# Gated cross-attention and ternary FFN on one core: 28 token tiles of 128, DMA transposes of heads and activations, half of the probability casts and the layernorm write on ScalarE, a hand-written opening order

## The chip, the cores and the metric

One core of one Trainium2 chip runs the whole program. The metric is the device time of one execution in microseconds (us); lower is better. The kernel before takes 1238.8 us, the median of 3 runs (1238.38 to 1241.94).

## The reference, cut to what matters

32 batches; in each, 112 query tokens `x` (256 wide) attend with 16 heads of 64 to 375 context tokens (256 wide). Then comes a feed-forward net with ternary weights and 8-bit activations, over tokens alone.

```
xn = layernorm(ctx) * w1 + b1;  k, v = split(xn @ Wkv)            # 375 x 2048 per batch
q  = (layernorm(layernorm(x)) * w2 + b2) @ Wq; q = q*(1+side) + side
p  = softmax(q k^T / 8);        x = x + tanh(g0) * ((p v) @ Wout) # 16 heads, 112 x 375
h  = act_quant(rmsnorm(layernorm(x))) @ ternary(W1)^T + b1        # 256 -> 1024
x  = x + tanh(g1) * (act_quant(rmsnorm(gelu(h))) @ ternary(W2)^T + b2)   # 1024 -> 256
```

Nothing behind the attention mixes tokens, so these 3584 tokens may be cut into tiles at any place.

## The kernel before, in words

Every float32 matmul operand is held as two float16 parts, a high one and the rest (`_h`, `_l`), and each product is three matmuls (`three`, L631). For each batch TensorE makes eight K jobs (128 rows of keys x 375), six V jobs (3 key tiles x 2 halves of 512 columns), two Q jobs, the transposes of the normalised inputs (Z0, Z1, ZX), eight score jobs S0 to S7 (two heads each, L644) and eight apply jobs A0 to A7 (probabilities times V, L656). Heads are transposed on TensorE (OO0, OO1) and go through Wout (WO); then the token steps follow: XT (transpose of the quantised x), F0 and F1 (first FFN layer), HT (transpose of the quantised hidden row), F2 (second layer). Each of the K, V, Q, Z, ZX, OO, WO, XT, HT and F jobs takes the next of four PSUM banks (`work`, `BANK` and `USE`).

Around them, for one pair of heads p: VectorE takes the row maximum (`M`, L561), ScalarE the exponential into float32 `prob` (`E`, L418), VectorE casts it to float16 into the first half of `pn` (`PH`, L568), GpSimd subtracts to get the low part (`PL`, L271), and SyncE issues one DMA transpose of `pn` (112 x 1536 float16) into `pt` (`T`, L211 to L217), which A of that pair reads. There are four `pn`/`pt` buffers and two of `prob`. The next S waits for E, since the score bank `ps_s` is single. K and V results leave PSUM in two steps: ScalarE writes the high part (`KH`, `VH`, L376), VectorE the low part (`KL`, `VL`, L498), and then the bank is free. GpSimd writes the layernorm result (`LNW`, L302 to L309) and splits q and z. Transposed heads leave PSUM through ScalarE (`OH`, L389) and VectorE (`OT`, L574); XT and HT leave through VectorE (`XTE`, `HTE`).

The order on each engine is a list written out by hand: `PE_ORDER`, `ACT_ORDER`, `DVE_ORDER`, `POOL_ORDER`, `SP_ORDER`, each a sequence of (step, batch offset) for one batch period, which `sequence` repeats for 32 batches with its ends cut off. All queues, SyncE's too, run strictly in their order: a step that waits holds everything behind it. Token steps run for each batch, that is for 32 tiles of 112 tokens, one to three periods behind the attention. Weight preparation (split in high and low, ternary rounding) is hung in front of named steps by `prepare` (L360, L474); GpSimd's `prepare_sides` (L259) waits for all small loads and for ScalarE's tanh.

Of the kernel before, what the change touches and what calls it, by code (L numbers as in the profile page):

```python
# [4 lines left out]
F16 = mybir.dt.float16  # L5
# [30 lines left out]
PE_ORDER = [  # L36
# [31 lines left out]
]  # L68

SP_ORDER = [  # L70
    ("T7", -1), ("T0", 0), ("T1", 0), ("T2", 0), ("LD", 3), ("T3", 0), ("T4", 0), ("RS", 0),
    ("T5", 0), ("ST", -3), ("T6", 0),
]
FIRST, LAST = -3, B + 2


def sequence(order):

    return [(name, it + off) for it in range(FIRST, LAST + 1) for name, off in order if 0 <= it + off < B]
# [3 lines left out]
for n, job in enumerate(j for j in sequence(PE_ORDER) if j[0][0] not in 'SA'):  # L83
    BANK[job], USE[job] = n % WORK_BANKS, n // WORK_BANKS + 1
HI_COUNT = {s: n + 1 for n, s in enumerate(s for s in sequence(ACT_ORDER) if s[0][0:2] in ("KH", "VH"))}


def build(nc, x, ctx, fside, g_x, g_f, ln1w, ln1b, ln2w, ln2b, wq, wkv, wout, w1, b1, w2, b2, out):
    from contextlib import ExitStack
    with ExitStack() as st:  # L90
# [13 lines left out]
        x1_b2 = stage[0:SQ, 0:B * D]  # L104
# [5 lines left out]
        ident, ident_h = sb("ident", [P, P]), sb("ident_h", [P, P], F16)  # L110
# [5 lines left out]
        b1_row, b2_row = sb("b1_row", [SQ, FF]), sb("b2_row", [SQ, D])  # L116
# [4 lines left out]
        ctx_bn, ctx_mv, ctx_ve, ctx_rs = sb("ctx_bn", [TP, TT, 6]), sb("ctx_mv", [TP, TT, 2]), sb("ctx_ve", [TP, TT]), sb("ctx_rs", [TP, TT])  # L121
        ctx_nm, ctx_nb = sb("ctx_nm", [TP, TT]), sb("ctx_nb", [TP, TT])
        x_bn, x_mv, x_ve, x_rs = sb("x_bn", [SQ, 6]), sb("x_mv", [SQ, 2]), sb("x_ve", [SQ, 1]), sb("x_rs", [SQ, 1])
        x_nm, x_nb = sb("x_nm", [SQ, 1]), sb("x_nb", [SQ, 1])
# [13 lines left out]
        ot_h, ot_l = sb("ot_h", [P, IC, SQ], F16), sb("ot_l", [P, IC, SQ], F16)  # L138

        x_res, x1 = sb("x_res", [SQ, D]), sb("x1", [SQ, D])  # L140
        x1_bn, x1_mv, x1_ve, x1_c = sb("x1_bn", [SQ, 6]), sb("x1_mv", [SQ, 2]), sb("x1_ve", [SQ, 1]), sb("x1_c", [SQ, 1])
        xc, xr, xq = sb("xc", [SQ, D]), sb("xr", [SQ, D]), sb("xq", [SQ, D], F16)
        amax1, clip1, inv1, qs1, deq1 = (sb(n, [SQ, 1]) for n in ("amax1", "clip1", "inv1", "qs1", "deq1"))
        xqt = sb("xqt", [P, KC, SQ], F16)
        hid_g = sb("hid_g", [SQ, FF])
        hid_r, hid = (stage[0:SQ, 8 * INNER + FF * i:8 * INNER + FF * (i + 1)] for i in range(2))
        hid_q = sb("hid_q", [SQ, FF], F16)
        ssq, inv_ff, eps_col, g_ms, g_ve, g_rs = (sb(n, [SQ, 1]) for n in ("ssq", "inv_ff", "eps_col", "g_ms", "g_ve", "g_rs"))
        amax2, clip2, inv2, qs2, deq2, deq2t = (sb(n, [SQ, 1]) for n in ("amax2", "clip2", "inv2", "qs2", "deq2", "deq2t"))
        hqt = sb("hqt", [P, FF // P, SQ], F16)  # L150
        y = sb("y", [SQ, D])
# [5 lines left out]

        wk_in, wv_in, wq_in, wout_in, w1_in, w2_in, ln_in, small_in = (sem(n) for n in ("wk_in", "wv_in", "wq_in", "wout_in", "w1_in", "w2_in", "ln_in", "small_in"))
        ctx_loaded, x_loaded, res_loaded, y_stored = (sem(n) for n in ("ctx_loaded", "x_loaded", "res_loaded", "y_stored"))

        consts_ready, gates_ready, side_ready, abs_ready, abs_summed, mean_ready = (sem(n) for n in (
            "consts_ready", "gates_ready", "side_ready", "abs_ready", "abs_summed", "mean_ready"))
        hi_split, lo_split, tern_rounded, tern_ready = (sem(n) for n in ("hi_split", "lo_split", "tern_rounded", "tern_ready"))
# [5 lines left out]
        ctx_stats, ctx_normed, z_ready = (sem(n) for n in ("ctx_stats", "ctx_normed", "z_ready"))  # L169
# [621 lines left out]
```

## Time and profile before

| | before |
|---|---|
| median of 3 runs | 1238.8 us |
| the profiled execution's own time | 1237.77 us |
| its span, first to last instruction | 1235.6 us |
| TensorE busy | 1131.4 us (92%) |
| VectorE busy | 1044.9 us (85%) |
| GpSimd busy | 875.2 us (71%) |
| ScalarE busy | 855.1 us (69%) |
| DMA transposes and loads (dynamic queue) | 118.42 MB, 53.4% of the 16 engines |
| mean granted TensorE clock | 0.98 |

Busy is the time in which at least one instruction of the engine ran. Matmuls are pipelined: one of 375 columns is shown with 0.32 us, while the next starts 0.16 us later, so the cost of a job on TensorE is read from start to start.

### The profile page before, as it was taken

The numbers are of one execution on the slowest core, as the hardware profiler recorded it, in microseconds if no ns is written. First come the engines' busy times: TensorE is split into PE (matmuls) and PEld (weight loads), VectorE is DVE, ScalarE is ACT, GpSimd is POOL, SyncE is SP. The second block draws the span as 40 slices with busy tenths as digits, with TensorE's granted clock in tenths as the row PEclk, the third lists the DMA queues.
The fourth block names the chain that finished last, engine by engine and source line by source line (L and its number), as shares of the span: only waits on it lengthen the run. The fifth ranks groups of instructions, "written<-read, shape, count | busy, mean of one in ns | idle before, by whom it ended". The sixth has DMA issues, their size and how long they took to land.

```text
span 1235.6 us, 32509 instructions
## 1 busy us (share of the span) xinstructions
PE 1131.4 (92%) x12354; PEld 768.6 (62%) x12354; DVE 1044.9 (85%) x2224; ACT 855.1 (69%) x1638; POOL 875.2 (71%) x1049
## 2 busy tenths in 40 slices
PE   2778999999999999999999999999999999999964
PEld 1455666666666666667666666766666666666643
DVE  2578898888888898888898888889888888998874
ACT  3455677777777677777777777777777777777742
POOL 4556787777777877777787777778777777877551
PEclk9899999999999999999999999999999999999986
DMA  8245554565555556554646565565655655464440
GB/s 255 44 89 85 99 87 99 102 102 95 109 93 96 91 103 102 97 110 90 104 85 103 100 102 105 93 106 88 100 101 103 98 103 94 87 104 90 85 89 11
DMA packets 381304, 120.48 MB, mean 98 GB/s; under 512 B 354976, under 2 KB 380016, under 8 KB 381152
## 3 DMA queue, kind: packets, MB, share of 16 engines
q1 hardware_dynamic: 381152, 118.42, 53.4%
q8 instruction: 99, 1.62, 0.6%
q14 instruction: 53, 0.43, 0.1%
HBM read 26.63 MB, written 3.67 MB: 25 GB/s over the span
## 4 chain that ended last, share of the span: by engine, by line
PE 44%; DVE 21%; ACT 11%; issue 10%; DVEq 6%; DMA 5%; POOL 3%; POOLq 1%; ACTq 0%
PE work L634 10%; PE work L636 9%; PE work L635 9%; PE ps_s L653 6%; DVE neg_max L561 5%; DMA pt<-pn 4%; DVE pn L568 4%; ACT prob L418 4%; PE ps_o L634 3%; ACT L418 2%; ACT k_h L376 2%; ACT hid_g L428 2%; DVEq L531 2%; DVE k_l L498 2%; PE ps_o L635 2%
## 5 line engine op out<-in xcount | busy, mean ns | idle before, releaser
L271 POOL TENSOR_TENSOR pn<-prob,pn 112x750 f16<-112x750 f32 x256 | 400.3, 1564 | 109.7 <-DVE pn L568 108.6
L418 ACT ACTIVATE prob<-ps_s,neg_max 112x375 f32<-112x375 f32 x512 | 266.0, 571 | 267.8 <-DVE neg_max L561 267.4
L561 DVE TENSOR_REDUCE neg_max<-ps_s 112x2 f32<-112x750 f32 x256 | 238.6, 932 | 17.1 <-PE ps_s L653 17.0
L568 DVE CAST pn<-prob 112x750 f16<-112x750 f32 x256 | 174.6, 682 | 67.0 <-ACT prob L418 66.8
L634 PE MATMUL work<-z,wkv_h 128*128 128x375 f16 x512 | 168.3, 329 | 37.2 <-DVE k_l L498 33.7
L634 PEld LDWEIGHTS ps_o<-v_h,pt 128*128 128x128 f16 (+1 forms) x1536 | 139.7, 97 | 87.9 <-issue 63.9
L634 PE MATMUL ps_o<-v_h,pt 128*128 128x65 f16 (+1 forms) x1536 | 171.8, 197 | 15.7 <-DMA pt<-pn 15.6
L635 PE MATMUL ps_o<-v_l,pt 128*128 128x65 f16 (+1 forms) x1536 | 169.8, 194 | 0.0
L636 PE MATMUL ps_o<-v_h,pt 128*128 128x65 f16 (+1 forms) x1536 | 168.5, 194 | 0.0
L636 PE MATMUL work<-z,wkv_l 128*128 128x375 f16 x512 | 167.1, 326 | 0.0
L635 PE MATMUL work<-z,wkv_h 128*128 128x375 f16 x512 | 166.8, 326 | 0.0
L376 ACT ACTIVATE k_h<-work 128x375 f16<-128x375 f32 x256 | 122.4, 493 | 37.2 <-PE work L636 37.0
L634 PE MATMUL work<-wkv_h,z 128*128 128x512 f16 (+1 forms) x384 | 146.2, 381 | 0.0
L635 PE MATMUL work<-wkv_l,z 128*128 128x512 f16 (+1 forms) x384 | 145.8, 380 | 0.0
L636 PE MATMUL work<-wkv_h,z 128*128 128x512 f16 (+1 forms) x384 | 145.7, 379 | 0.0
L636 PEld LDWEIGHTS ps_o<-v_h,pt 128*128 128x128 f16 (+1 forms) x1536 | 144.5, 98 | 0.0
L635 PEld LDWEIGHTS ps_o<-v_l,pt 128*128 128x128 f16 (+1 forms) x1536 | 144.1, 99 | 0.0
L498 DVE SCALAR_TENSOR_TENSOR k_l<-work,k_h 128x375 f16<-128x375 f32 x256 | 135.7, 541 | 9.4 <-ACT k_h L376 5.4
L498 DVE SCALAR_TENSOR_TENSOR v_l<-work,v_h 128x512 f16<-128x512 f32 (+1 forms) x192 | 131.9, 687 | 1.9 <-ACT v_h L376 0.3
L334 POOL TENSOR_TENSOR stage<-x,b_row 112x256 f32<-112x256 f32 x32 | 23.4, 732 | 143.3 <-DVE x L591 143.3
L376 ACT ACTIVATE v_h<-work 128x512 f16<-128x512 f32 (+1 forms) x192 | 112.6, 605 | 10.6 <-PE work L636 9.4
L653 PE MATMUL ps_s<-k_h,q_h 64*112 64x375 f16 x512 | 94.1, 364 | 17.6 <-ACT prob L418 17.1
(131 smaller groups left out, 2924.2 us busy)
## 6 DMA issues: line engine op xcount, KB each, us to landing
ctx_in<-in_ctx SPq DMA_DIRECT2D x32, 375.0 KB
pt<-pn SPq DMA_TRANSPOSE x256, 3.5
x_in<-in_x SPq DMA_DIRECT2D x32, 112.0 KB, 5.7
x_res<-in_x SPq DMA_DIRECT2D x32, 112.0 KB, 2.2
out<-y SPq DMA_DIRECT2D x32, 112.0 KB, 2.6
stage<-in_wkv SPq DMA_DIRECT2D x2, 1024.0 KB, 9.5
stage<-in_w SPq DMA_DIRECT2D x2, 1024.0 KB, 12.2
stage<-in_wq SPq DMA_DIRECT2D x1, 1024.0 KB, 9.3
```

What stands on the lines that cost most here:

```text
L271: g.tensor_tensor(pn[p % PBUF][:, 1, :, 0:SK], prob[:, p % 2], pn[p % PBUF][:, 0, :, 0:SK], ALU.subtract).then_inc(p_lo, 1)
L376: a.activation(dst, src, ACT.Identity, scale=1.0 / W_SCALE).then_inc(hi_done, 1)
L418: i = a.activation(prob[:, p % 2, h, :], ps_s[0:SQ, h, 0:SK], ACT.Exp, bias=neg_max[:, h:h + 1])
L428: a.activation(hid_g[:], hid[:], ACT.Gelu).then_inc(gelu_done, 1)
L498: v.scalar_tensor_tensor(out=dst, in0=src, scalar=1.0 / W_SCALE, in1=hi_part, op0=ALU.mult, op1=ALU.subtract).then_inc(evacuated[BANK[job] ...
L531: dve.drain()
L561: v.tensor_reduce(neg_max[:], ps_s[0:SQ, :, 0:SK], X, ALU.max, negate=True).then_inc(max_ready, 1)
L568: v.tensor_copy(pn[p % PBUF][:, 0, :, 0:SK], prob[:, p % 2]).then_inc(p_hi, 1)
L634: t_.matmul(dst, sh, mh, start=(n == 0), stop=False)
L635: t_.matmul(dst, sh, ml, start=False, stop=False)
L636: i = t_.matmul(dst, sl, mh, start=False, stop=(n == len(pairs) - 1))
L653: i = t_.matmul(ps_s[0:SQ, h, 0:SK], q[r, p, :], k[r, p, :], start=(n == 0), stop=(n == 2))
```

## The change

It does five things.

1. The token steps (RS, WO, X1 to YE, ST) run on 28 tiles of 128 rows, cut from the 3584 tokens without regard to the batch. `sequence` leaves out every eighth. `x_rows` and `out_rows` are the flat views; all `[SQ, ...]` tiles of these steps become `[P, ...]`.
2. The jobs OO0, OO1, XT and HT on TensorE are gone. ScalarE casts the heads from `attn` to `an` (`OH`), GpSimd subtracts the low part (`OL`), SyncE transposes both parts by DMA (`OT`) into a ring of 896 columns `ot_h`, `ot_l`. The quantised x and hidden tiles are transposed by DMA too (`XD`, `HD`), and VectorE clips them from SBUF to SBUF.
3. The casts `PH` of the pairs 0, 2, 4 and 6 run on ScalarE, those of 1, 3, 5 and 7 stay on VectorE.
4. The layernorm write `LNW` (three rows of 256 for the context, one for x) runs on ScalarE; GpSimd's power and product for context and x are one instruction each in place of two (`LNA`).
5. Each engine gets a list `FIRST` of its own for the opening, about two batches long, in which weight preparation and small constants are steps with a place of their own (`WKH`, `WQL`, `AS0`, `TN0`, `GT`, `SUM`, ...); then the new list `ORDER` repeats. In the opening SyncE loads Wk ahead of the small vectors and Wq ahead of the sides; gates and FFN biases are loaded with batch 1.

```diff
+NT = B * SQ // P
+RING = 7 * P
+CAST_ACT = (0, 2, 4, 6)
+ORDER["PE"] = [
+    ("Z1", 1), ("K5", 0), ("V00", 0), ("S0", 0), ("K7", 0), ("A4", -1), ("V02", 0), ("V01", 0),
+    ("A5", -1), ("S1", 0), ("K0", 1), ("A6", -1), ("Q1", 0), ("A7", -1), ("S2", 0), ("K1", 1),
+    ("V10", 0), ("ZX", 1), ("F0", -2), ("S3", 0), ("K2", 1), ("V11", 0), ("K3", 1), ("S4", 0),
+    ("F1", -2), ("A0", 0), ("A1", 0), ("V12", 0), ("K4", 1), ("S5", 0), ("WO", -1), ("A2", 0),
+    ("S6", 0), ("Q0", 1), ("A3", 0), ("F2", -3), ("Z0", 2), ("S7", 0), ("K6", 1),
+]
+ORDER["ACT"] = [
+    ("HR", -3), ("E0", 0), ("XR", -2), ("VH02", 0), ("KH7", 0), ("VH01", 0), ("PH0", 0), ("KH0", 1),
+    ("E1", 0), ("QF1", 0), ("KH1", 1), ("E2", 0), ("VH10", 0), ("ZXF", 1), ("OH1", -1), ("PH2", 0),
+    ("KH2", 1), ("E3", 0), ("VH11", 0), ("LNW", 2), ("KH3", 1), ("E4", 0), ("GE", -2), ("E5", 0),
+    ("PH4", 0), ("KH4", 1), ("VH12", 0), ("SQ", -2), ("E6", 0), ("QF0", 1), ("ZF0", 2), ("KH6", 1),
+    ("PH6", 0), ("E7", 0), ("KH5", 1), ("VH00", 1), ("OH0", 0), ("ZF1", 2),
+]
...
+ORDER["SP"] = [
+    ("XD", -2), ("T0", 0), ("T1", 0), ("OT0", -1), ("OT1", -1), ("LD", 3), ("T2", 0), ("ST", -4),
+    ("RS", -1), ("T3", 0), ("T4", 0), ("T5", 0), ("T6", 0), ("T7", 0), ("HD", -2),
+]
...
+    return [(name, b - b // 8 - 1 if name in TOKEN_STEPS else b) for name, b in steps if b % 8 or name not in TOKEN_STEPS]
...
+            def turn_heads(b, half):
+                sp.wait_ge(o_lo, 2 * b + half + 1)
...
+                for dst, part in ((ot_h, 0), (ot_l, 1)):
+                    sp.dma_start_transpose(dst[:, 4 * half:4 * half + 4, columns(b)],
+                                           an[half][:, part]).then_inc(o_turned[half], 16)
+            def turn_quantised(t):
+                sp.wait_ge(xq_ready, t + 1)
...
+                sp.dma_start_transpose(xqt_r[:], xq[:]).then_inc(x_turned, 16)
+            def turn_hidden(t):
+                sp.wait_ge(hq_ready, t + 1)
...
+                sp.dma_start_transpose(hqt_r[:], hid_q[:]).then_inc(h_turned, 16)
...
+            def split_heads(b, half):
+                pool.wait_ge(o_hi, 2 * b + half + 1)
+                g.tensor_tensor(an[half][:, 1], attn[:, half * HALF:(half + 1) * HALF], an[half][:, 0], ALU.subtract).then_inc(o_lo, 1)
...
+                    for t in range(TT):
+                        a.activation(ctx_n[:, t, :], ctx_in[:, t, :], ACT.Identity, bias=ln_nb[0:TP, t:t + 1], scale=ln_rs[0:TP, t:t + 1])
...
+                if name[0:2] == "PH":
...
+                    act.wait_ge(exp_done, g + 1)
...
+                    a.activation(pn[p % PBUF][:, 0, :, 0:SK], prob[:, p % 2], ACT.Identity).then_inc(p_hi_act, 1)
...
-                if name in ("OO0", "OO1"):
-                    pe.wait_ge(o_normed, 2 * b + 1 + int(name[2]))
-                    for m in range(4):
-                        c = 4 * int(name[2]) + m
-                        i = t_.transpose(w[:, m * SQ:(m + 1) * SQ], attn[:, c * P:(c + 1) * P], ident[0:SQ, 0:SQ])
```

## Rows read from the trace of the kernel before

**Rows 1.** Busy time by stage: engine busy us (instructions), granted clock, DMA share, GB/s.

```profile
0.00:49.50 49.50, 18.67 (x99) 10.28 (x100) 16.91 (x42) 15.77 (x25) 24.34 (x53) 0.90 0.57 172
49.50:128.00 78.50, 64.45 (x667) 41.50 (x666) 62.34 (x109) 44.32 (x90) 48.18 (x53) 0.96 0.49 83
128.00:1203.70 1075.70, 1033.11 (x11507) 705.33 (x11504) 951.11 (x2037) 785.75 (x1513) 797.48 (x935) 1.00 0.56 98
1203.70:1235.60 31.90, 15.18 (x89) 11.52 (x86) 14.50 (x37) 9.21 (x11) 5.17 (x9) 0.61 0.04 11
```

**Rows 2.** The same view for one period; order PE, PEld, DVE, ACT, POOL.

```profile
469.87:505.52 35.65, 34.72 (x388) 23.73 (x386) 31.61 (x70) 26.40 (x51) 27.04 (x33) 1.00 0.61 99
```

**Rows 3.** TensorE's waits between 128 and 1203 us: total us, times, longest.

```profile
PE work L634 <- DVE k_l L498: 22.3, 28, 1.7
PE ps_o L634 <- DMA pt<-pn: 15.6, 12, 3.2
PE ps_s L653 <- ACT prob L418: 4.3, 6, 1.4
```

**Rows 4.** TensorE's instructions in order of time, around 505 us: start, length, line.

```profile
500.13 0.55 PE L714 MATMUL work<-ident,attn 112*128 112x112 f32 x4
500.60 0.37 PE L653 MATMUL ps_s<-k_h,q_h 64*112 64x375 f16 x2
...
501.78 0.62 PE L734 MATMUL work<-w_t,xqt 128*112 128x512 f16 x2
502.23 0.32 PE L634 MATMUL work<-z,wkv_h 128*128 128x375 f16 x1
...
504.49 0.56 PE L727 MATMUL work<-ident_h,hid_q 112*128 112x112 f16 x8
504.97 0.37 PE L653 MATMUL ps_s<-k_h,q_h 64*112 64x375 f16 x2
...
506.15 0.29 PE L634 MATMUL work<-wout_h,ot_h 128*112 128x256 f16 x1
...
508.79 1.04 PE L740 MATMUL work<-w_t,hqt 128*112 128x256 f16 x8
509.76 0.37 PE L653 MATMUL ps_s<-k_h,q_h 64*112 64x375 f16 x2
```

**Rows 5.** ScalarE's instructions in order of time.

```profile
508.82 0.60 ACT L376 ACTIVATE v_h<-work 119x512 f16<-119x512 f32 x1
509.30 1.07 ACT L431 ACTIVATE stage<-hid_g 112x1024 f32<-112x1024 f32 x1
510.25 0.21 ACT L431 ACTIVATION_READ_ACCUMULATOR stage<-hid_g 112x1 f32 x1
...
526.67 0.60 ACT L422 ACTIVATE xr<-xc,round_col,qs 112x256 f32<-112x256 f32 x1
527.16 0.48 ACT L376 ACTIVATE k_h<-work 128x375 f16<-128x375 f32 x1
```

**Rows 6.** Two of VectorE's casts in order of time.

```profile
513.27 1.29 DVE L568 CAST pn<-prob 112x750 f16<-112x750 f32 x1
...
523.72 0.55 DVE L568 CAST pn<-prob 112x750 f16<-112x750 f32 x1
```

**Rows 7.** Groups of instructions: count, then busy us, mean ns, idle before.

```profile
L271 POOL TENSOR_TENSOR pn<-prob,pn 112x750 f16<-112x750 f32 x256 | 400.3, 1564 | 109.7 <-DVE pn L568 108.6
...
L568 DVE CAST pn<-prob 112x750 f16<-112x750 f32 x256 | 174.6, 682 | 67.0 <-ACT prob L418 66.8
...
L574 DVE TENSOR_TENSOR ot_l<-work,ot_h 128x448 f16<-128x448 f32 x64 | 39.3, 614 | 0.6 <-ACT ot_h L389 0.6
```

**Rows 8.** The tile pt: its DMA transposes, from issue to landing.

```profile
DMA to landing us min/median/max: 3.4/3.5/7.6
```

**Rows 9.** The page's DMA issues: KB each, median us from issue to landing.

```profile
x_res<-in_x SPq DMA_DIRECT2D x32, 112.0 KB, 2.2
```

**Rows 10.** The row maxima of all pairs: first and last start.

```profile
L561 DVE TENSOR_REDUCE neg_max<-ps_s x256: 921/929/941, 49.5 to 1194.8; 112x2 f32<-112x750 f32 x128
```

**Rows 11.** The chain that ended last, in the opening.

```profile
37.02 6.33 DMA ctx_in<-in_ctx
```

More of the change, by code:

```diff
@@ new lines, in sequence, with last_batch, columns, last_user @@
+def sequence(engine):
+    done = set(FIRST[engine])
+    steps = FIRST[engine] + [(name, it + off) for it in range(START, END) for name, off in ORDER[engine]
+                             if 0 <= it + off < B and (name, it + off) not in done]
+    return [(name, b - b // 8 - 1 if name in TOKEN_STEPS else b) for name, b in steps if b % 8 or name not in TOKEN_STEPS]
+def last_batch(t):
+    return (t * P + P - 1) // SQ
+def columns(b):
+    return slice(b * SQ % RING, b * SQ % RING + SQ)
+def last_user(b):
+    return [((b - 7) * SQ - 1) // P] if b >= 8 else []
@@ L88, in build @@
+CAST_COUNT = {(b, p): sum((i in CAST_ACT) == (p in CAST_ACT) for i in range(PAIRS)) * b
+              + sum((i in CAST_ACT) == (p in CAST_ACT) for i in range(p + 1)) for b in range(B) for p in range(PAIRS)}
 def build(nc, x, ctx, fside, g_x, g_f, ln1w, ln1b, ln2w, ln2b, wq, wkv, wout, w1, b1, w2, b2, out):
@@ L103, in build @@
         w2_f = stage[:, 10 * INNER:12 * INNER].rearrange("p (k n) -> p k n", k=FF // P)
-        x1_b2 = stage[0:SQ, 0:B * D]
+        RC = IC * RING // 2
+        ot_h, ot_l = (stage[:, RC * i:RC * (i + 1)].bitcast(F16).rearrange("p (c q) -> p c q", c=IC) for i in range(2))
+        x1_b2 = stage[:, 2 * RC:2 * RC + 4 * D].rearrange("p (s d) -> p s d", s=4)
+        hid_r, hid = (stage[:, 8 * INNER + FF * i:8 * INNER + FF * (i + 1)] for i in range(2))
         wkv_h, wkv_l = sb("wkv_h", [P, KC, 2 * INNER], F16), sb("wkv_l", [P, KC, 2 * INNER], F16)
@@ L235, in _ @@
                     store(b)
-            sp.wait_ge(y_stored, 16 * B)
+            sp.wait_ge(y_stored, 16 * NT)
         @block.gpsimd
@@ L386, in step @@
                 if name[0:2] == "OH":
[L387 to L390 removed]
+                    half = int(name[2])
+                    act.wait_ge(o_normed, 2 * b + half + 1)
+                    if b > 0:
+                        act.wait_ge(o_turned[half], 32 * b)
+                    a.activation(an[half][:, 0], attn[:, half * HALF:(half + 1) * HALF], ACT.Identity).then_inc(o_hi, 1)
                 if name[0:2] == "QF":
                     half = int(name[2])
+                    if b == 0:
+                        act.wait_ge(side_ready, 1)
                     act.wait_ge(full[BANK[job]], USE[job])
@@ L410, in step @@
                     i.then_inc(evacuated[BANK[job]], 1)
+                if name == "LNW":
+                    act.wait_ge(ln_ready, b + 1)
+                    if b > 0:
+                        for n in ("Z0", "Z1", "ZX"):
+                            act.wait_ge(full[BANK[n, b - 1]], USE[n, b - 1])
+                    for t in range(TT):
+                        a.activation(ctx_n[:, t, :], ctx_in[:, t, :], ACT.Identity, bias=ln_nb[0:TP, t:t + 1], scale=ln_rs[0:TP, t:t + 1])
+                    a.activation(x_n[:], x_in[:], ACT.Identity, bias=ln_nb[0:SQ, TT:TT + 1],
+                                 scale=ln_rs[0:SQ, TT:TT + 1]).then_inc(ctx_normed, 1)
                 if name[0] == "E":
@@ L461, in weight_means @@
             def weight_means():
-                dve.wait_ge(abs_summed, 1)
-                v.tensor_scalar(w_mean[:], ps_o[:, 0, 4 * VW:4 * VW + 2], 1.0 / (FF * D), 1e-5, ALU.mult, ALU.max)
+                bank = BANK["SUM", 0]
+                dve.wait_ge(full[bank], USE["SUM", 0])
+                v.tensor_scalar(w_mean[:], work[:, bank, 0:2], 1.0 / (FF * D), 1e-5, ALU.mult, ALU.max).then_inc(evacuated[bank], 1)
                 dve.drain()
@@ L715, in job @@
                 if name == "WO":
                     if b == 0:
-                        pe.wait_ge(lo_split, 4)
-                    results(b, ["OO0", "OO1"])
-                    i = three(w[0:SQ, 0:D], [(ot_h[:, c, :], ot_l[:, c, :], wout_h[:, c, :], wout_l[:, c, :]) for c in range(IC)])
-                if name == "XT":
-                    pe.wait_ge(xq_ready, b + 1)
-                    for c in range(KC):
-                        i = t_.transpose(wh[:, c * SQ:(c + 1) * SQ], xq[:, c * P:(c + 1) * P], ident_h[0:SQ, 0:SQ])
@@ L724, in job @@
-                if name == "HT":
-                    pe.wait_ge(hq_ready, b + 1)
-                    for c in range(FF // P):
-                        i = t_.transpose(wh[:, c * SQ:(c + 1) * SQ], hid_q[:, c * P:(c + 1) * P], ident_h[0:SQ, 0:SQ])
+                        pe.wait_ge(lo_split[3], 1)
+                    for half in range(2):
+                        pe.wait_ge(o_turned[half], 32 * (last_batch(b) + 1))
+                    r = slice(b % (RING // P) * P, (b % (RING // P) + 1) * P)
@@ L728, in job @@
+                    i = three(w[:, 0:D], [(ot_h[:, c, r], ot_l[:, c, r], wout_h[:, c, :], wout_l[:, c, :]) for c in range(IC)])
                 if name in ("F0", "F1"):
                     if b == 0:
-                        pe.wait_ge(tern_ready, 1)
-                    results(b, ["XT"])
+                        pe.wait_ge(tern_ready[0], 1)
+                    pe.wait_ge(x_clipped, b + 1)
                     c = slice(int(name[1]) * HALF, (int(name[1]) + 1) * HALF)
                     for k in range(KC):
-                        i = t_.matmul(w[0:SQ, :], xqt[:, k, :], w1_t[:, k, c], start=(k == 0), stop=(k == KC - 1))
+                        i = t_.matmul(w[:, :], xqt[:, k, :], w1_t[:, k, c], start=(k == 0), stop=(k == KC - 1))
```

407 lines of the change are left out of this document (212 added, 195 removed), and 70 rows, old and new, of tables (ACT_ORDER, CAST_ACT, DVE_ORDER, PE_ORDER).

## The prediction, made before the changed kernel was run

> **What bounds it now.** I cut the span into stages first, with the view of busy time by stage. Between 128 and 1203.7 us the kernel repeats 30 like periods, 1075.7 / 30 = 35.86 us each; ahead of them lie an opening of 49.5 us (to the first row maximum) and the first two batches with 78.5 us, behind them a tail of 31.9 us [rows 1, 10]. In the periods TensorE is busy 1033.11 / 30 = 34.44 us, at a granted clock of 1.00; in one typical period it is 34.72 of 35.65, against 31.61 for VectorE, 27.04 for GpSimd and 26.40 for ScalarE [rows 1, 2]. So TensorE is the bound, and not by appearance: its jobs stand start to start. The view of waits gives the remainder, 42.2 us in all or 1.4 us per period: 22.3 for VectorE's late low part of a K result, 15.6 for late transposes of probabilities, 4.3 for the exponential [rows 3]. The reader should see that the repeated part is worth 30 times whatever leaves TensorE, while opening and tail are chains of their own, in which TensorE works less than half the time.
>
> **TensorE's part.** From start to start [rows 4]: the transposes of one half of the heads take 500.60 - 500.13 = 0.47 us, two per batch 0.94; those of the hidden row 504.97 - 504.49 = 0.48; the two of the quantised x, by the same rate, 0.12. These 1.54 us go for every batch. WO takes 508.79 - 506.15 = 2.64 us, F2 0.97, F0 and F1 0.45 each: 4.51 us for a token tile. The 24 matmuls of WO take 0.11 us each for 256 columns, those of F0 0.225 for 512 [rows 4]: the time goes by the columns streamed, so I take a tile of 128 rows to cost what one of 112 does. One tile in eight is saved: 0.56 us per batch. Together 2.10 us; TensorE's need falls from 34.44 to 32.34 us per period.
>
> **The waits.** VectorE loses four of eight casts, 4 x 0.68, and two subtractions for the heads, 2 x 0.61 [rows 7]: 31.61 - 3.9 = 27.7 us of work, 83% of the new period, so the largest wait, for the low part of K, should shrink. What I set against it are ScalarE's new load and more transposes in SyncE's queue, so I let the wait fall only from 1.4 to 1.2 us. Period: 33.5 us. 30 x (35.86 - 33.5) = 71 us less; I round to 70. Bounds: waits of 0.4 us give 93 us less; waits of 2.4 us give 33 less.
>
> **ScalarE's part.** A cast of 750 elements lies between the 512-element row (start to start 0.48 us) and the 1024-element one (0.95) [rows 5]: 0.70 us, four times 2.8. The layernorm write is four rows of 256 with scale and bias per row, like the 0.49 us of `xr` [rows 5]: 2.0. The high part of the heads stays about what it was, and an eighth of the token steps goes, under 1 us. 26.40 + 4.8 - 0.8 = 30.4 us, bounds 29.5 (casts at 0.48) and 31.2 (no token steps saved): 88 to 93% of 33.5. It costs nothing in the sum as long as it hides under TensorE; it is the closest second, and the first rival.
>
> **GpSimd's part.** It gives up the layernorm write and gets two subtractions of 512 elements, at most 1.56 us each [rows 7]: 27.04 + 3.1 = 30.2 at the very most, still under 33.5. Nothing in the sum.
>
> A row bears on the casts: the same cast takes 0.55 us at 523.72 and 1.29 us at 513.27, where GpSimd's subtraction was running [rows 6]; the mean of 0.68 [rows 7] holds some of that, and ScalarE's copy should be free of it. The Trainium skill, in "SBUF — State Buffer", on the shared port pair, says that VectorE and GpSimd take one pair of ports as an exclusive lock and the loser blocks for the whole instruction, while ScalarE has its own. By that rule the trace's long casts are lock waits, and half of them go; this is the mechanism of the third rival, below.
>
> **DMA.** Eight pair transposes per period read 112 x 1536 float16 = 344 KB each, 2752 KB. Added are heads, 4 x 115 KB, and per token tile 66 and 262 KB, times 7/8: 746 KB, or 27% more. The DMA share of 0.56 [rows 1], all of it taken as transposes, becomes at most 0.56 x 1.27 x 35.9 / 33.5 = 0.76. Room is left. SyncE's queue is in order: XD stands ahead of T0 and waits for GpSimd's quantised x, the OTs stand ahead of T2 and wait for GpSimd's low part of the heads, HD stands behind T7 and waits for a GpSimd step of the next period, ahead of XD. Queued behind each are the pair transposes and the loads. Each A comes about four score jobs behind its T, some 16 us at 8 scores per period, less 3.2 us for maximum, cast and subtraction [rows 7, 10] and the exponential, against 3.5 us to landing [rows 8]; that cover hides the waits. If it is gone, a late landing costs TensorE its full delay (second rival below).
>
> **Opening.** Now VectorE stands at a statistic of batch 2 for 6.33 us while the load lands, and the first maxima wait behind it [rows 11]; the new order puts that step behind the first maximum. The layernorm write, Wq and the small loads leave the chain as well. I take 8.5 us (bounds 6, nothing but that wait, and 15). The first two batches take 78.5 us, 6.8 more than two periods [rows 1]; with new periods of 33.5, half of that excess kept, they take 70.4, 8 less (bounds 4.7 and 12). Together 16.5.
>
> **Tail.** Behind the last attention the three transposes by DMA stand in a serial chain. No row shows a small transpose; the nearest are 2.2 us to landing for a plain 112 KB load [rows 9] and 3.5 us for a pair transpose [rows 8]. I take 2.8 each, 8.4 us, and 1.2 for the new subtraction on GpSimd, less the TensorE transposes, which at the tail's clock of 0.61 take near twice the 1.07 us of one half of the heads, x and hidden, and less 0.6 for VectorE's subtraction: 9.6 - 2.0 - 0.6 = 7, bounds 5 and 10. The Trainium skill, "DMA: Bandwidth & Descriptors", in the anatomy of one DMA, gives a fixed part of about 2.0 us for any transfer; an estimate by it, 2.0 plus 115 KB at 436 GB/s, is 2.3 us a hop, and the sum would be 1.6 us lower. It speaks against small transposes on a serial path, and the trace of before, without any, can't say.
>
> **Sum.** 1237.8 (the profiled execution's own time: span 1235.6 and 2.2 around it) - 70 - 16.5 + 7 = 1158 us. That execution lies 1 us under the median of the runs; I forecast 1159.
>
> **Rivals.**
> - *ScalarE becomes the bound.* For: 30.4 us of work, two in-order queues (maximum, exponential) answering one another eight times per period; each exponential still waits for its maximum, as it waits now. If 4.2 us of idle time stay (half a microsecond per pair), the period is 34.6: 30 x 1.26 = 38 less, 1237.8 - 38 - 9.5 = 1190. Against: TensorE waits for the exponential 4.3 us in all now [rows 3], and a seventh more work need not change that.
> - *Slower than before.* SyncE's queue: XD, OT or HD waits for GpSimd, and the pair transposes behind it land late. The worst landing now is 7.6 us instead of 3.5 [rows 8]. Were one per period late on the path by these 4.1 us on top of the forecast, the period is 37.6 and the time 1237.8 + 30 x 1.74 - 9.5 = 1280. It decides the sign from 2.7 us per period on. Against: four buffers and a cover of over 10 us.
> - *The waits nearly vanish.* VectorE and GpSimd no longer collide in half of the casts, VectorE has 17% to spare; the waits fall to 0.4 us: 1237.8 - 93 - 9.5 = 1135.
> - *The repeated part does not move.* Another chain (maximum, exponential, cast, subtraction, transpose, apply) sets the period and only the opening pays: about 1228. Against: TensorE stands still for 1.4 us of 35.9 only.
>
> **Chances.** Forecast 0.61, ScalarE 0.18, waits vanish 0.13, does not move 0.04, slower 0.04. The forecast's own bounds are about 1145 to 1175. The range reaches down to 1134, through the third rival, and up to 1194, through the first. About 0.3% (4 us) is what a measurement of this kernel can tell from no change; faster takes all cases but the last and a sliver of the one before it.
>
> **What would show it.** Right: periods of 33.5 us with TensorE over 95% busy in them, no L714-like transposes of heads; the low-part wait under 15 us in all; first maximum near 41 us; ScalarE at 30 us per period; DMA share near 0.7; tail near 39 us. Wrong: TensorE's waits on ScalarE's exponential or on bank releases over 2 us per period (first rival), waits on `pt` that repeat in every period (second), or a period above 35 with TensorE under 93% busy.

## The result and the profile after

The changed kernel takes 1320.72 us (median of the runs, 1319.58 to 1324.64) against 1238.62 us for the kernel before beside it: ratio 1.066, interval 1.063 to 1.069. It is slower by 82 us; 1159 was forecast. The profiled execution has a span of 1317.8 us, against 1235.6.

The view of busy time by stage of the changed kernel, cut at the same places as [rows 1] (opening to the first row maximum, first two batches, repeated part, tail), with one late period in the last row but one; columns are the stretch, its length, busy us and instructions of PE, PEld, DVE, ACT and POOL, the granted clock, the DMA share and GB/s:

```profile
0.00:37.40 37.40, 17.05 (x99) 9.90 (x100) 17.01 (x36) 20.27 (x31) 16.15 (x37) 1.00 0.72 229
37.40:101.70 64.30, 57.22 (x593) 35.30 (x591) 52.29 (x93) 52.77 (x107) 44.50 (x43) 0.97 0.48 96
101.70:1277.10 1175.40, 1035.48 (x10890) 687.25 (x10888) 827.61 (x1754) 894.59 (x1718) 778.77 (x808) 0.94 0.57 109
1189.90:1224.70 34.80, 32.43 (x363) 21.46 (x363) 26.96 (x51) 28.41 (x55) 23.89 (x26) 1.00 0.54 114
1277.10:1317.80 40.70, 12.97 (x56) 7.08 (x56) 13.17 (x36) 9.30 (x11) 7.04 (x11) 0.58 0.18 43
```

| us | before | forecast | after |
|---|---|---|---|
| opening, to the first row maximum | 49.5 | 41.0 | 37.4 |
| first two batches | 78.5 | 70.4 | 64.3 |
| one period (of 30) | 35.86 | 33.5 | 39.18 |
| tail | 31.9 | 38.9 | 40.7 |

So the opening and the first two batches gave 26 us, 10 more than forecast; the tail took 9; and the repeated part, where 71 us were to be gained, lost 1175.4 - 1075.7 = 100 us. The question is the period alone. No engine has more work than was reckoned: per period VectorE is busy 27.6 us (forecast 27.7), ScalarE 29.8 (30.4), GpSimd 26.0 (30.2 at most). TensorE is the exception, 1035.48 / 30 = 34.5 us where 32.3 were forecast, with 617 fewer instructions than before and a clock of 0.94. And it waits. TensorE's waits in the repeated part, as in [rows 3] (total us, times, longest):

```profile
PE ps_o L765 <- DMA pt<-pn: 114.7, 30, 6.7
PE work L765 <- DMA stage<-an: 12.5, 16, 2.0
PE work L765 <- DVE k_l L616: 8.4, 19, 1.1
PE ps_s L784 <- ACT prob L551: 1.2, 1, 1.2
```

VectorE's late low part went from 22.3 to 8.4 us, the exponential from 4.3 to 1.2, as the forecast hoped. The wait for turned probabilities went from 15.6 us in 12 pieces to 114.7 in 30: once per period, 3.8 us. Instruction by instruction, 27 of the 30 stand ahead of the same job, A2, one in each of the batches 2 to 28. SyncE's queue in one period shows why:

```profile
583.55 1.23 SPq L327 DMA_TRANSPOSE hqt_r<-hid_q  x1
584.88 1.21 SPq L321 DMA_TRANSPOSE xqt_r<-xq  x1
586.78 6.13 SPq L304 DMA_TRANSPOSE pt<-pn  x2
593.00 5.80 SPq L314 DMA_TRANSPOSE stage<-an  x4
598.86 0.47 SPq L288 DMA_DIRECT2D ctx_in<-in_ctx  x1
599.37 0.53 SPq L289 DMA_DIRECT2D x_in<-in_x  x1
600.00 3.28 SPq L304 DMA_TRANSPOSE pt<-pn  x1
```

The order is T0 and T1, then the four transposes of the heads, the load of the next context and x, then T2. Each transpose of the heads holds the queue about 1.3 us, although it moves only 115 KB; T2 itself, right behind the load, holds it 3.28 us, where a pair transpose takes 1.34 in the median elsewhere. GpSimd has the low part of pair 2 ready well before that:

```profile
592.90 1.57 POOL L389 TENSOR_TENSOR pn<-prob,pn 112x750 f16<-112x750 f32 x1
```

It ends at 594.5; T2 is issued at 600.0. The chain of work that ended last goes the same way, and gives the second half of the delay (start, length, what):

```profile
591.58 1.33 SPq L304
593.00 1.21 SPq L314
...
600.00 6.46 DMA pt<-pn
...
638.56 7.12 DMA pt<-pn
```

The transposes of the other pairs take 3.1 to 4.3 us to landing; this one takes 6.46, and the one of the next batch 7.12. The table gives the median time from issue to landing of each pair's transpose, over the middle batches, worked out from the traces:

```
us        T0    T1    T2    T3    T4    T5    T6    T7   the load stands ahead of
before    3.5   3.5   3.5   5.7   4.5   3.5   3.5   3.5  T3
after     3.1   3.3   6.5   3.9   4.3   4.0   3.1   3.1  T2
```

[Rows 8] showed a median of 3.5 us and a worst of 7.6; sorted by place, the bad ones sit behind the 487 KB load. Third part: what the wait does to TensorE. The same view by stage, in small steps around the stall:

```profile
602.00:604.00 2.00, 0.89 (x9) 0.55 (x6) 0.73 (x2) 2.00 (x5) 0.65 (x1) 1.00 1.53 182
604.00:606.50 2.50, 0.00 (x1) 0.01 (x1) 0.00 (x0) 1.17 (x3) 2.43 (x2) 0.94 0.82 229
606.50:608.00 1.50, 1.50 (x22) 1.31 (x24) 0.00 (x0) 0.00 (x0) 0.75 (x2) 0.50 1.26 287
608.00:610.00 2.00, 2.00 (x24) 1.46 (x21) 1.17 (x2) 0.20 (x1) 0.00 (x0) 0.59 1.55 208
610.00:612.00 2.00, 2.00 (x39) 1.91 (x36) 1.83 (x5) 2.00 (x6) 0.00 (x0) 1.00 0.50 108
...
648.00:650.00 2.00, 2.00 (x25) 2.00 (x24) 1.95 (x4) 0.97 (x2) 0.00 (x0) 0.50 1.13 76
```

TensorE stands from about 603 to 606.5. When it starts again the granted clock is 0.50, the 1.2 GHz level, and it is back at 1.00 only after about 3 us; in the next period it starts again at 645.7 and is still at 0.50 from 648 to 650 (last row). So a stall costs its length and some work at half speed behind it. Wait and slow clock account for the period: 34.5 busy, and 139.5 / 30 = 4.65 of waits, is 39.2; of the 34.5, 2.2 are above the forecast and 1.8 above the 32.75 us that TensorE needs in the fastest kernel below, at a clock of 1.00.

One stall shows the wait by itself. Each row below runs from one start of A2 to the next, with one wait of 3.6 to 4.0 us in it. The first begins with a slow stretch. The second begins behind a wait of 3.46 us after which the clock stayed at 1.00, the only one of the 27:

```profile
606.50:645.70 39.20, 34.83 (x368) 22.98 (x368) 28.44 (x62) 30.89 (x59) 26.70 (x29) 0.94 0.64 115
884.33:922.85 38.52, 33.53 (x369) 21.95 (x369) 27.66 (x62) 30.83 (x59) 26.92 (x30) 1.00 0.56 113
```

TensorE is busy for 33.5 us there and for 34.8 with the slow stretch, with as many matmuls; in the other periods with a token tile it is 34.0 to 36.4. So even at full clock the period is far above the forecast: the wait is the larger part, and the clock adds up to 3 us.

One more thing speaks for the load as a partner: the last batches have nothing left to load. The row 1189.90:1224.70 above is a stretch of that kind: 34.80 us, 4.4 shorter than the mean period, at a clock of 1.00, TensorE busy for 32.43 of it, with the heads' transposes still in the queue. From first row maximum to first row maximum the periods of batches 29 and 30 take 34.6 and 34.7 us, and neither has a wait for turned probabilities.

### The profile page after: what moved, and what is told of

Its sections match the earlier page's. It is cut to its first block, busy times and chain, and to the rows that moved or that the text cites. A ratio compares the mean times of both kernels' runs of the same rounds, so it can differ in the third digit from the quotient of the medians.

```text
span 1317.8 us, 31456 instructions
## 1 busy us (share of the span) xinstructions
PE 1122.7 (85%) x11634; PEld 739.5 (56%) x11634; DVE 910.1 (69%) x1916; ACT 976.9 (74%) x1866; POOL 846.5 (64%) x897
## 4 chain that ended last, share of the span: by engine, by line
PE 34%; POOL 15%; DMA 12%; issue 9%; SPq 9%; DVE 7%; POOLq 6%; ACT 5%; DVEq 2%; ACTq 0%
DMA pt<-pn 11%; PE work L765 7%; SPq L314 7%; PE work L766 7%; PE work L767 7%; PE ps_s L784 6%; POOL pn L389 5%; POOLq L413 3%; PE ps_o L765 2%; POOL q_l L401 2%; POOL z L414 2%; POOL an L394 2%; PE ps_o L766 2%; PE ps_o L767 2%; ACT prob L551 2%
## 5 line engine op out<-in xcount | busy, mean ns | idle before, releaser
L765 PE MATMUL ps_o<-v_h,pt 128*128 128x65 f16 (+1 forms) x1536 | 180.2, 202 | 119.2 <-DMA pt<-pn 117.2
L765 PEld LDWEIGHTS ps_o<-v_h,pt 128*128 128x128 f16 (+1 forms) x1536 | 151.9, 102 | 140.9 <-DMA pt<-pn 123.1
L766 PE MATMUL ps_o<-v_l,pt 128*128 128x65 f16 (+1 forms) x1536 | 180.1, 200 | 0.0
L767 PE MATMUL ps_o<-v_h,pt 128*128 128x65 f16 (+1 forms) x1536 | 179.7, 201 | 0.0
L766 PEld LDWEIGHTS ps_o<-v_l,pt 128*128 128x128 f16 (+1 forms) x1536 | 151.6, 104 | 10.9
L767 PEld LDWEIGHTS ps_o<-v_h,pt 128*128 128x128 f16 (+1 forms) x1536 | 151.8, 102 | 0.0
L616 DVE SCALAR_TENSOR_TENSOR k_l<-work,k_h 128x375 f16<-128x375 f32 x256 | 138.4, 541 | 17.3 <-ACT k_h L477 16.9
L616 DVE SCALAR_TENSOR_TENSOR v_l<-work,v_h 128x512 f16<-128x512 f32 (+1 forms) x192 | 128.2, 681 | 1.2 <-ACT v_h L477 0.7
L477 ACT ACTIVATE v_h<-work 128x512 f16<-128x512 f32 x192 | 116.3, 606 | 6.3 <-PE work L767 4.0
L561 ACT ACTIVATE pn<-prob 112x750 f16<-112x750 f32 x128 | 106.9, 835 | 0.1
L441 POOL TENSOR_TENSOR x_c<-x_ve,minus_half 128x1 f32<-128x1 f32 x28 | 16.4, 587 | 139.7 <-DVE x_ve L647 139.7
L517 ACT ACTIVATE q_f<-work,side_add,side_mul 128x112 f32<-128x112 f32 x256 | 92.9, 446 | 14.5 <-PE work L767 14.5
```

What stands on the lines that cost most here:

```text
L477: a.activation(dst, src, ACT.Identity, scale=1.0 / W_SCALE).then_inc(hi_done, 1)
L517: i = a.activation(q_f[:, c, :], work[:, BANK[job], m * SQ:(m + 1) * SQ], ACT.Identity, bias=add, scale=mul)
L561: a.activation(pn[p % PBUF][:, 0, :, 0:SK], prob[:, p % 2], ACT.Identity).then_inc(p_hi_act, 1)
L616: v.scalar_tensor_tensor(out=dst, in0=src, scalar=1.0 / W_SCALE, in1=hi_part, op0=ALU.mult, op1=ALU.subtract).then_inc(evacuated[BANK[job] ...
L765: t_.matmul(dst, sh, mh, start=(n == 0), stop=False)
L766: t_.matmul(dst, sh, ml, start=False, stop=False)
```

## The experiments

All times are medians beside runs of the kernel before on the same chip (1236.8 to 1237.8 us). Period, opening and tail come from each trace, cut at the same events. The queue's list, SyncE's, is the place of most edits; the order of the changed kernel is `T0 T1 OT0 OT1 LD T2 ST RS T3 ...`. Rows of waits are cut at fixed times: 128 to 1270 us in the first and third run, 101 to 1270 in the second (SyncE's row), 128 to 1203 in the fourth, 104 to 1140 with the load split or late, 101 to 1120 in the last kernels. In the slower kernels they leave out one to five of the last periods.

**Which of the two steps ahead of T2: the load or the heads?** First only the load goes behind T2.

```diff
-("OT0", -1), ("OT1", -1), ("LD", 3), ("T2", 0),
+("OT0", -1), ("OT1", -1), ("T2", 0), ("LD", 3),
```

> The changed kernel with one move in SyncE's repeated list: the load of the batch three ahead (LD) goes behind the transpose T2 instead of ahead of it. Theory 1 (order in SyncE's queue): T2, which A2 waits for, is issued 6 us after its data are there and then lands in 6.5 us because 487 KB of load are under way; with LD behind it, it is issued 1 us sooner and lands in about 3.5, so the 3.8 us wait of TensorE ahead of A2 goes, and the period falls from 39.5 to about 35: some 1185 us, faster than both kernels. Theory 2 (the DMA engines or SyncE's queue have too much work in sum, 27% more transposed bytes): the order does not matter, over 1290 us. Theory 3 (ScalarE is overloaded, so everything on TensorE comes late): no change either, over 1290 us.

Measured: 1330.2 us, ratio 1.076 (1.074 to 1.078), period 39.46. Nothing gained. TensorE's waits in its repeated part, and from TensorE's timeline the instruction behind one of them (start, length, line, and in brackets the idle time before it):

```profile
PE ps_o L765 <- DMA pt<-pn: 118.0, 31, 5.8
```

```profile
614.87 0.23 PE L765 MATMUL ps_o<-v_h,pt 128*128 128x65 f16 x1 [5.25 <-DMA pt<-pn]
```

T2 now lands in 3.1 us, but T3, now right behind the load, in 7.1, and TensorE waits ahead of A3 instead of A2. The victim is whichever transpose follows the load.

Then both the load and T2 ahead of the heads:

```diff
-("OT0", -1), ("OT1", -1), ("LD", 3), ("T2", 0),
+("LD", 3), ("T2", 0), ("OT0", -1), ("OT1", -1),
```

> The changed kernel with LD ahead of T2 as it is, but the four transposes of the heads (OT0, OT1) behind T2. Theory 1, if the heads' transposes are what holds T2: T2 is issued some 3 to 5 us sooner, though still behind the load, and lands in 6.5 us; TensorE's wait ahead of A2 shrinks by about 3 us: period 36.5, some 1230 us. LD itself waits for the layernorm write of ScalarE, which may hold T2 in its turn. If the load's traffic is the larger part, this run gains less than the one with LD behind T2. Theory 2 and 3: over 1290 us.

Measured: 1419.52 us, ratio 1.147 (1.143 to 1.152), period 42.28. Worse, and the DMA queue's own waits, then TensorE's (104 to 1373 us), show why:

```profile
SPq L288 <- ACT x_n L542: 79.8, 27, 3.7
```

```profile
PE work L765 <- DMA stage<-an: 192.7, 27, 8.5
```

Moved forward, the load itself waits 3 us per period for ScalarE to have done with the input buffer (the layernorm write), which I had overlooked in the edit, and T2 and the heads stand behind it. T2 still lands in 6.6 us, but TensorE hardly waits for it any more (22.5 us in 9 pieces for all pairs): it waits ahead of WO for the heads. Two moves are mixed in this run, so it doesn't price either alone.

And T2 ahead of both:

```diff
-("OT0", -1), ("OT1", -1), ("LD", 3), ("T2", 0),
+("T2", 0), ("OT0", -1), ("OT1", -1), ("LD", 3),
```

> The changed kernel with T0, T1, T2 first, then the heads' transposes, then LD. Theory 1: T2 lands well before A2; but now the heads' transposes are issued 3 us later and WO, which stands ahead of A2 on TensorE, may wait for them instead: between 1175 (no new wait) and 1230 us (WO waits 1.5 us per period). Theory 2 and 3: over 1290 us.

Measured: 1321.69 us, ratio 1.069 (1.065 to 1.072), period 39.07. No gain:

```profile
PE work L765 <- DMA stage<-an: 83.6, 26, 4.7
PE ps_o L765 <- DMA pt<-pn: 39.2, 24, 4.9
```

Now the heads are late for WO, which is in TensorE's queue ahead of A2, and T3 lands in 6.2 us behind the load. In these three runs the loss only moved, or grew. None of the three orders of these steps helps: T2, T3 and the heads are each needed by TensorE soon.

**Does the load alone do it, without the rest of the change?** The kernel before, with the load one place earlier, ahead of T2 as in the changed one.

```diff
-("T1", 0), ("T2", 0), ("LD", 3), ("T3", 0),
+("T1", 0), ("LD", 3), ("T2", 0), ("T3", 0),
```

> The kernel before with LD moved ahead of T2, as the change has it, nothing else. If the load ahead of T2 alone costs the time, whatever stands in the queue besides, this is slower by over 2 us per period (over 1300 us). If it takes the heads' transposes in front of it too, there is room for it here: T2 then lands a few us later, still in time for A2: within 1% of 1238 us.

Measured: 1400.36 us, ratio 1.132 (1.130 to 1.134), period 41.13, and T2 lands in 6.4 us. The DMA queue's waits, then TensorE's:

```profile
SPq L204 <- POOL x_n L309: 178.6, 26, 7.2
```

```profile
PE ps_o L634 <- DMA pt<-pn: 119.3, 26, 5.2
```

One place of one step costs the kernel before 163 us, though here two things add: the load waits for the buffer (6.9 us each time, 26 times), so T2 is issued 4.6 us after its data (median), and T2 lands late behind it. No part of the change's new work is needed for this kind of stall.

**Is it the load's shape?** The context tile has 125 partitions, all transposes have 112. The load is split in 112 and 13 partitions, same bytes, same place (shortened; VectorE's wait for the load counts both parts).

```diff
-sp.dma_start(ctx_in[:], rows)
+sp.dma_start(ctx_in[0:SQ], rows[0:SQ])
+sp.dma_start(ctx_in[SQ:TP], rows[SQ:TP])
```

> The changed kernel with nothing moved: only the context load of 125 partitions is cut into two, 112 and 13 partitions. The runs so far say that a pair transpose issued right behind a load lands in 6.3 to 7.1 us instead of 3.1, wherever in the list that is. Theory 1a (the load's own time on the DMA engines is what the next transpose waits for, and it is long because 125 partitions spread over few engines): spread over more engines, the transpose T2 behind it lands in some 4.5 us, TensorE waits 2 us less ahead of A2 and keeps its clock: period 39.5 to about 37, some 1245 us. Theory 1b (the load is bound by memory or by its bytes, not by how it is spread): T2 still lands in 6.5 us, within 1% of 1320 us.

Measured: 1241.42 us, ratio 1.004 (1.002 to 1.006), period 36.78: 79 us less than the changed kernel, from one more DMA per batch. Some 72 of them are the period's, the rest the opening and the first two batches. T2 lands in 3.9 us instead of 6.5. What is left:

```profile
PE ps_o L770 <- DMA pt<-pn: 70.3, 39, 5.4
PE work L770 <- DMA stage<-an: 14.7, 18, 1.4
```

The Trainium skill, in "DMA: Bandwidth & Descriptors", on why a DMA increments its semaphore by 16, says that a transfer is dealt to the largest number of engines up to 16 that divides the slowest dimension of both its sides. By that rule 125 partitions go to 5 engines, 112 to 16 and 13 to 13. The traces agree. T2 lands in 6.5 us behind the whole load and in 3.9 behind the split one. And the packets of 1024 bytes, which are the rows of the two loads and of x, can be counted by their starts and durations: in the 9 us behind the issue of the whole load, the commonest number of them under way at once, while any is, is 5, in the kernel before and in the changed one; behind the split load it is 16.

The same split in the kernel before:

> The kernel before with its context load cut in the same way (112 and 13 partitions). There T3 stands behind the load and lands in 5.7 us, with room ahead of A3. Theory 1a: T3 lands in about 4.5 us and the time stays within 0.5% of 1238 us, since TensorE hardly waits for transposes there (15.6 us in all, of which some may go). Theory 1b: no change in landing.

Measured: 1226.5 us, ratio 0.992 (0.990 to 0.993). T3 lands in 4.0 us instead of 5.7, but the period goes only from 35.86 to 35.74; most of the 10 us come from the opening (49.5 to 42.7), where the first maxima waited for a load [rows 11]. In the kernel before the late T3 was just hidden: in the median it landed 0.2 us ahead of A3.

**Somewhere with more cover.** The load goes behind T4, three pairs later, with T2 and T3 ahead of it.

```diff
-("LD", 3), ("T2", 0), ("ST", -4), ("RS", -1), ("T3", 0), ("T4", 0), ("T5", 0),
+("T2", 0), ("ST", -4), ("RS", -1), ("T3", 0), ("T4", 0), ("LD", 3), ("T5", 0),
```

> The changed kernel with LD moved behind T4, to where no pair transpose is due for some 5 us; the load itself is unchanged. Theory 1 (a load just ahead of a transpose that TensorE is about to need): T2, T3 and T4 all land in about 3.1 us, T5 has its data later than the load's end; TensorE's wait on pt falls from 3.8 to under 1 us per period, its clock stays at 2.4 GHz, the period is about 34.5: some 1170 us. Theory 2 (too many transposes in sum) and 3 (ScalarE): over 1270 us.

Measured: 1240.61 us, ratio 1.002 (1.000 to 1.004), period 36.53. T5 behind the load takes 7.0 us, yet TensorE's wait for probabilities is down to 13.4 us. Another took its place: TensorE's waits, and VectorE's wait for the load.

```profile
PE work L765 <- DVE k_l L616: 41.5, 28, 3.0
PE work L765 <- DMA stage<-an: 22.5, 23, 1.6
PE ps_o L765 <- DMA pt<-pn: 13.4, 10, 3.2
```

```profile
DVE ln_bn L706 <- DMA ctx_in<-in_ctx: 75.1, 27, 4.9
```

Loaded this late, the context arrives after VectorE has come to its statistics; VectorE stands 2.8 us and the low part of K behind it is late. A faster load should cure just that, so both edits together:

> Both: LD behind T4 and the context load cut in two. Theory 1: as with LD behind T4 alone, or up to 1% less, since T5 may still meet the load's tail; some 1165 us.

Measured: 1184.05 us, ratio 0.958 (0.956 to 0.960), period 34.86. The view by stage, a stretch of 33.5 us in its middle with as many matmuls as a mean period (363), and TensorE's waits:

```profile
500.00:533.50 33.50, 32.66 (x363) 21.40 (x360) 25.72 (x61) 28.91 (x57) 26.28 (x28) 1.00 0.59 122
```

```profile
PE work L770 <- DMA stage<-an: 23.0, 23, 2.0
PE ps_o L770 <- DMA pt<-pn: 14.4, 12, 3.4
PE work L770 <- DVE k_l L621: 7.3, 13, 1.4
```

VectorE's wait for the load is 23.6 us. What remains first is the heads' transposes.

**The issue cost of the heads.** Both parts of a half are made one tile of 112 x 1024 and turned by one DMA instead of two (the ring of the transposed heads and the indices of WO follow).

```diff
-for dst, part in ((ot_h, 0), (ot_l, 1)):
-    sp.dma_start_transpose(dst[:, 4 * half:4 * half + 4, columns(b)],
-                           an[half][:, part]).then_inc(o_turned[half], 16)
+sp.dma_start_transpose(ot[:, 8 * half:8 * half + 8, columns(b)],
+                       an[half][:].rearrange("p a k -> p (a k)")).then_inc(o_turned[half], 16)
```

On top of the last kernel:

> On top of the kernel with LD behind T4 and the context load in two parts (1184 us): the high and the low part of a half of the heads are transposed by one DMA of 112 x 1024 instead of two of 112 x 512, so two issues per period in place of four. SyncE's queue spent 1.2 to 1.4 us on each transpose, small ones too (1.20 for 256 columns, 1.36 for 1536). If that issue time is fixed, T2 and the heads each get 2.5 us sooner, and TensorE's remaining waits (23 us for heads, 14 for pairs) shrink: 1165 to 1175 us. If the issue time goes by the bytes, or the queue is no longer what holds TensorE, within 0.5% of 1184 us.

Measured: 1163.11 us (1162.35 to 1163.45), ratio 0.939 (0.938 to 0.941), period 34.14. It is the fastest kernel of the study. The view by stage of its repeated part, the heads in SyncE's queue (3.4 us where it was 5.8), and TensorE's waits, whose heads line fell from 23.0 to 1.6 us:

```profile
101.00:1120.00 1019.00, 977.36 (x10830) 641.83 (x10829) 791.28 (x1741) 887.94 (x1713) 767.75 (x804) 1.00 0.61 125
```

```profile
519.01 3.42 SPq L322 DMA_TRANSPOSE stage<-an  x2
522.52 1.37 SPq L313 DMA_TRANSPOSE pt<-pn  x1
```

```profile
PE work L773 <- DVE k_l L624: 13.2, 18, 1.6
...
PE ps_o L773 <- DMA pt<-pn: 7.1, 8, 2.3
...
PE work L773 <- DMA stage<-an: 1.6, 3, 0.6
```

The same merge alone, in the changed kernel with the load as it was:

> The changed kernel itself with nothing moved and the load whole, only the heads' transposes merged two into one. It prices the queue's issue time in the changed kernel: T2 stands behind four issues of heads (5.4 to 5.8 us) and the load. With two issues it is issued 2.5 us sooner, unless it then waits for its own data; it still lands behind the load in 6.5 us. Wait ahead of A2 3.8 - 2.5 = 1.3 us, period about 36.5, some 1235 us. If only the load's traffic counts, over 1300 us.

Measured: 1229.47 us, ratio 0.993 (0.991 to 0.996), period 36.27. Two issues fewer per period are worth 91 us there, although T2 still lands in 6.6 us: it is issued some 2.4 us sooner, the wait shrinks from 114.7 to 69.9 us in all, and the mean granted clock rises from 0.93 to 0.96.

**Was it ScalarE?** It was my first rival, so the fast kernel was needed to test it. In the version with split and late load, all casts go back to VectorE (`CAST_ACT = ()`, the four steps into VectorE's list).

> On the same 1184 us kernel (without the merged transposes), the casts of pairs 0, 2, 4 and 6 go back to VectorE, each just ahead of the next maximum. Theory ScalarE (its 29 us of work per period are what keeps the period at 34.8 instead of 33.5): the period falls, under 1170 us. Theory of the forecast (ScalarE hides under TensorE, and VectorE's relief pays for the low parts of K): VectorE gets 4 x 0.7 us back and is late again with the low parts: slower by 0.5 to 2%, 1190 to 1210 us.

Measured: 1187.07 us (1183.17 to 1195.0), ratio 0.960 (0.955 to 0.965), against 0.958 with the casts shared: not to be told apart. The costliest groups with casts shared, then with all on VectorE:

```profile
L566 ACT ACTIVATE pn<-prob 112x750 f16<-112x750 f32 x128 | 106.7, 834 | 0.1
L705 DVE CAST pn<-prob 112x750 f16<-112x750 f32 x128 | 85.7, 669 | 19.7 <-ACT prob L556 19.6
```

```profile
L705 DVE CAST pn<-prob 112x750 f16<-112x750 f32 x256 | 204.6, 799 | 33.2 <-ACT prob L556 32.7 <-issue 0.2
```

ScalarE doesn't set the period in this version (the changed kernel itself was not run so), and moving the casts, a part of the change that looks like relief, brought nothing measurable in time. The casts left on VectorE take 0.67 us on the mean, against 0.68 in the kernel before [rows 7] and 0.80 with all eight there in the new order: of the shorter casts that the third rival hoped for, next to nothing came, beside the time of the four that went.

**The order of WO and A2.** In the fastest kernel TensorE takes A2 ahead of WO.

```diff
-("S5", 0), ("WO", -1), ("A2", 0),
+("S5", 0), ("A2", 0), ("WO", -1),
```

> The merged kernel with A2 ahead of WO on TensorE instead of behind it: WO's heads get 0.6 us more, A2's transpose has 2.6 us less. If the remaining waits are for heads, 0.5% faster than the merged kernel; if T2 has little room, slower by up to 2%, since A2 then waits for T2 in most periods, which would show how near to its limit the changed kernel's order is.

Measured: 1171.95 us (1165.02 to 1175.78), ratio 0.946 (0.942 to 0.950), against 0.939 without the swap. Slower: the wait for probabilities goes from 7.1 to 13.8 us. The change's order, WO first, is the better one here: its 2.6 us are cover for T2.

## Why the prediction was wrong

- **TensorE's need** nearly held. 34.44 - 2.10 = 32.34 us was forecast; the repeated part of the fastest kernel, at a clock of 1.00, shows 977.36 us for 1019.0 / 34.14 = 29.85 periods, 32.75 each. So 1.7 of the 2.1 us came from the 28 tiles and the jobs taken off TensorE; where the other 0.4 went was not looked for.
- **VectorE, ScalarE, GpSimd** held in their sums. A cast on ScalarE took 0.83 us where 0.70 was interpolated.
- **Opening and first two batches**: 26 us gained, 16.5 forecast (bounds 10.7 and 27). **Tail**: 8.8 us, 7 forecast (5 to 10). The small transposes land in 2.4, 2.3 and 3.2 us in the median of the run, 2.8 was taken for each; the lower 2.3 that the prediction set beside it fits the first two.
- **The step that failed** stands in the part on DMA: "Each A comes about four score jobs behind its T, some 16 us ... that cover hides the waits." The cover itself was counted too long. In the list of the kernel before, three score jobs stand between S and A of a pair, not four; in the changed one it is four, three or two, for pair 2 three. Its trace, for one pair (the subtraction, the issue of T, the first matmul of A):

```profile
512.60 1.56 POOL L271 TENSOR_TENSOR pn<-prob,pn 112x750 f16<-112x750 f32 x1
...
514.18 1.36 SPq L216 DMA_TRANSPOSE pt<-pn  x1
...
520.34 0.20 PE L634 MATMUL ps_o<-v_h,pt 128*128 128x65 f16 x1
```

  The data are ready at 514.2, T lands 3.5 us later and A starts 2.7 us after that. Over the middle batches each A starts 5.9 to 8.4 us after its data, by place, and 0.2 (A3) to 4.5 us after the landing. The "cover of over 10 us" was nowhere in it; the room beyond a landing of 3.5 us was about 3 us. In the changed kernel's order A2 comes 8.5 us after its data when it doesn't wait (medians with the load late).

  Against that room three terms were left out. First, T2 stands in the queue not behind its own data but behind four issues of the heads and two of the load: 5.8 and 1.0 us here, so it starts 5.6 us after its data. I had asked of OT and XD only whether they wait for GpSimd, and counted their bytes (27% more, harmless; the DMA share of the repeated part is 0.57), never the time that each issue holds the queue. Second, the landing was taken as 3.5 us in every place, while that behind the load took 5.7 in the kernel before, and the change moves the load ahead of T2: 6.5. Together 12.1 us against 8.5, which leaves 3.6 us of wait; 3.7 is the median measured. Third, TensorE's clock: the forecast priced a late landing at "its full delay"; it costs 3.8 us of waits and about 1.8 us of slow work per period.
- **The rival that came** was the "slower" one, SyncE's queue with one pair transpose per period late: 37.6 us per period and 1280 us, at a chance of 0.04. Its place and its rate were right; its reason was right in part only. It let XD, OT or HD wait for GpSimd, but in the whole run SyncE waits 2.6 us for the low parts of the heads, 1.9 us for the quantised x and 46.1 us for the hidden row, and the last doesn't delay T0, which is issued as soon as its data are there. What holds T2 is the time of the issues and the load. It was priced too low, by the clock, and I held it off with "four buffers and a cover of over 10 us", which I had not checked along the queue or against the trace. The point from which it decides the sign, 2.7 us a period, was passed by 3.
- **ScalarE as the bound** fell (casts on either engine: same time). **The waits nearly vanish** fell too: with the stall mended, (1019.0 - 977.36) / 29.85 = 1.4 us of each period are still not TensorE's, as before; I forecast 1.2. **The repeated part does not move** fell with the period of 34.14.
- With the stall mended, by edits to the queue's order, the load and the heads' transposes, the change takes 1163.11 us; 1159 was forecast. That they lie so close is luck in part: opening and first two batches are some 15 us shorter than forecast, 30 periods of 34.14 instead of 33.5 some 19 us longer, and the tail 2 us.

Each part of T2's delay is shown by a run that takes it away or shortens it: the load's shape 79 us, its place 80, half of the heads' issues 91. They don't add (both load edits 137, all three 158), since each removes part of one stall, which ends when A2's data is there. The clock's share was not taken away by an edit; it rests on the one stall without a slow stretch and on the busy times, 34.5 against 32.75 us per period. That the new tiles or the layernorm write, each alone, pay for themselves was not tried.

## What to carry to other kernels

An in-order DMA queue is an engine: sum the issue time of each entry (here 1.2 to 1.4 us for a transpose of 66 to 344 KB) between the moment at which data is ready and its own entry, and do it for each step that is moved or added, before trusting a cover counted in the consumer's jobs. Read the cover itself from the trace, from the data's end to the consumer's start: counted from the list it came out four jobs instead of three here. Read landings by their place in the queue, not by the median of the group; the outliers point at the transfer ahead of them, and a tile of 125 partitions was worth splitting. When a reorder gains nothing, look whether the wait moved to the neighbour (A2, A3, WO in turn), and if so shorten the transfers or merge them instead.

## What the runs showed of the hardware

- A DMA transpose holds SyncE's queue for nearly the same time whatever its size, if nothing is in its way: in the median 1.20 us for the quantised x (66 KB), 1.26 for 112 x 512, 1.25 for 112 x 1024, 1.34 for 112 x 1536. Right behind the whole load of 125 partitions the last of these takes 3.3 us. Two issues fewer per batch were worth 91 us in the changed kernel (1320.7 to 1229.5) and 21 us in the one with split and late load (1184.1 to 1163.1).
- A pair transpose issued right behind the 375 KB load of 125 partitions and the 112 KB of x lands in 5.7 us in the kernel before and in 6.2 to 7.1 in the runs with another order of the queue, against 3.1 to 3.5 us in most other places; behind the same bytes in 112, 13 and 112 partitions in 3.9 to 4.0.
- After 26 of 27 waits of 3.0 to 6.7 us ahead of A2, TensorE's granted clock was at 0.50, the 1.2 GHz level, for part of the work behind; in one period for 3 us, in the next for over 4. After one wait of 3.46 us it stayed at 1.00.
- From issue to landing, medians: 2.4 us for one transpose of the heads (115 KB), 2.3 for the quantised x (66 KB), 3.2 for the hidden row (262 KB).
